# Clears and weight pieces moved within the second attention, and score products made twice in half of its maxima pass

## The reference, cut to what matters

```python
h = h + _L1_attn_ref(_layernorm(h), W_attn, b_attn, P_q, P_k, P_v, W_back, W_proj, b_proj)
h = h + _L1_ffn_ref(_layernorm(h), Wr, W1, b1, W2, b2, sW1, sb1, sW2, sb2)
# attention: 12 heads of 8, causal
qkv = x @ W_attn + b_attn; q, k, v = split(qkv); q = q @ P_q; k = k @ P_k; v = v @ P_v
w = softmax(mask(q @ k.T / sqrt(8))); out = (w @ v) @ W_back @ W_proj + b_proj
# experts: 8 experts (192 -> 768 -> 192), top 2 of them for each token, and a shared one
```

## Time and profile before

| | us |
|---|---|
| median of the runs (3) | 943.63 |
| lowest, highest | 940.45, 945.43 |
| the profiled execution, its own time | 941.8 |
| its span in the trace | 939.9 |
| TensorE busy | 687.7 (73%) |
| VectorE busy | 648.5 (69%) |
| ScalarE busy | 647.2 (69%) |
| GpSimd busy | 315.0 (34%) |

### The profile page before, as it was taken

One profiled execution on the slowest core, in us unless ns is written; L12 is line 12 of the kernel. 1 busy time (PEld: TensorE's weight loads), 2 busy tenths in 40 slices (PEclk: granted clock), 3 DMA queues, 4 the chain that ended last, 5 costly groups with the idle time before them and its releaser, 6 DMA issues. The chain is left out here.

```text
span 939.9 us, 19804 instructions
## 1 busy us (share of the span) xinstructions
PE 687.7 (73%) x7422; PEld 517.9 (55%) x7423; DVE 648.5 (69%) x1374; ACT 647.2 (69%) x1225; POOL 315.0 (34%) x252
## 2 busy tenths in 40 slices
PE   2586472344199555989999939745985898999995
PEld 2563240122177323479999924333554567999994
DVE  3478998999679888955454455467669885554542
ACT  1568955999799686876556437889774752977672
POOL 6730750000000000067887442510002102678854
PEclk9887555555599776999999969765997899999998
DMA  6444772000032224933443261830554942334432
GB/s 200 145 89 119 242 252 52 0 17 9 3 110 93 93 84 147 331 90 69 64 59 54 31 205 56 312 110 3 201 209 150 339 179 75 59 59 64 60 39 30
DMA packets 61367, 105.78 MB, mean 113 GB/s; under 512 B 9709, under 2 KB 43128, under 8 KB 61032
## 3 DMA queue, kind: packets, MB, share of 16 engines
q1 hardware_dynamic: 44904, 88.19, 28.2%
q0 software_dynamic: 16384, 16.53, 11.4%
HBM read 76.91 MB, written 27.77 MB: 111 GB/s over the span
## 5 line engine op out<-in xcount | busy, mean ns | idle before, releaser
L2414 DVE SCALAR_TENSOR_TENSOR m_hT<-m_pu,m_unit,m_hT 128x512 f16<-128x512 f32 (+1 forms) x138 | 86.3, 663 | 21.5 <-ACT m_hT L2370 21.5
L1140 ACT ACTIVATE a_ex<-m_pieces,a_nb 128x256 bf16<-128x256 f16 x192 | 94.3, 492 | 5.4 <-DVE a_nb L1166 5.4
L2377 ACT ACTIVATE m_pu<-m_pu,m_b,m_unit 128x256 f32<-128x256 f32 (+1 forms) x138 | 63.7, 507 | 45.0 <-PE m_pu L2284 43.1
L2406 DVE COPY m_xgT<-m_px 128x768 f16<-128x768 f16 (+1 forms) x46 | 22.9, 497 | 102.9 <-PE m_px L2252 100.2
L979 PE MATMUL a_pp<-a_room 16*128 16x256 bf16 x240 | 56.1, 412 | 39.4 <-DVE m_pieces L1154 31.9
L2370 ACT ACTIVATE m_hT<-m_pu,m_unit 128x512 f16<-128x512 f32 (+1 forms) x138 | 81.3, 634 | 0.0
L2213 POOL DMA_INDIRECT m_xg<-xn_d,m_token x70 | 68.9, 984 | 32.3 <-issue 19.4
L2381 ACT ACTIVATE m_pu<-m_pu,m_unit 128x512 f32<-128x512 f32 (+1 forms) x69 | 41.1, 596 | 52.0 <-PE m_pu L2284 51.9
L2225 POOL DMA_INDIRECT out_h<-m_yo,m_token x39 | 62.1, 1592 | 31.6 <-DVE m_yo L2424 12.0
L2225 POOL DMA_INDIRECT h_d<-m_yo,m_token x39 | 62.1, 1591 | 25.5 <-issue 9.7
L2284 PE MATMUL m_pu<-m_xgT,m_pieces 128*128 128x256 f16 (+1 forms) x690 | 69.3, 260 | 0.9 <-DVE m_xgT L2406 0.9
(11 more groups left out here) (492 smaller groups left out, 1691.1 us busy)
## 6 DMA issues: line engine op xcount, KB each, us to landing
m_pieces<-in_m_w SPq DMA_DIRECT2D x11, 768.0 KB, 5.0
a_early_w<-in_m_w SPq DMA_DIRECT2D x10, 768.0 KB, 5.5
hv_raw<-in_m_w SPq DMA_DIRECT2D x8, 768.0 KB, 8.1
w1h_d<-hv_parts SPq DMA_DIRECT2D x8, 768.0 KB, 5.0
m_w<-w1h_d SPq DMA_DIRECT2D x8, 768.0 KB, 9.4
m_pieces<-in_m_w SPq DMA_DIRECT2D x8, 576.0 KB, 5.9
a_room<-in_m_w SPq DMA_DIRECT2D x8, 576.0 KB
hv_raw<-in_m_w SPq DMA_DIRECT2D x8, 576.0 KB, 7.8
```

Source lines behind the costliest of these rows:

```text
L1140: last = act.activation(ex[:, n % 2, r], v16t[:, n, r, :], ACT.Exp, bias=nbt[:, n, r:r + 1], scale=scale, accum_out=sumst[:, n, r:r + 1])
L2377: act.activation(pu[:, u, n, q * w:(q + 1) * w], pu[:, u, n, q * w:(q + 1) * w], ACT.Relu, bias=b1[:, bass.ds(e * FC + 2 * n + q, 1)], sca ...
L2414: last = v.scalar_tensor_tensor(hT[:, u, 1, third], pu[:, u, n, 0:2 * w], unit[:, 1:2], hT[:, u, 0, third], ALU.mult, ALU.subtract)
```

## The change

1. The third clear of `vv` waits for `normed` at 8 and no longer at 12.
2. FRONT - 1 becomes FRONT in the projection block: store, fetch and GpSimd's `low` of piece 6 (and the fetch of piece 10) move there from the maxima block, `low` of piece 6 ahead of `weigher.reduce`.
3. In the maxima block, units 12 to 23 make the 8 score products twice; the second set starts over, so the result is the same.
4. In the context block VectorE splits pieces 7 and 8 ahead of its wait for the turned late rows, and SyncE stores them (and fetches 11 and 12) ahead of `put_rows` and `take_rows`. The splits of pieces 9 to 15 stand behind the division of images 0 to 6 and no longer between the copy and the division.

```diff
-    COUNT, FRONT, RAW, PARTS = 2 * E, 7, 4, 3
+    COUNT, FRONT, MIXED, RAW, PARTS = 2 * E, 7, 9, 4, 3
...
-                        for n in range(Halves.FRONT - 1):
+                        for n in range(Halves.FRONT):
                             halves.store(sp, n)
                             halves.fetch(sp, n + 4)
...
-                            pool.wait_ge(normed, 4 * k + 4)
+                            pool.wait_ge(normed, min(4 * k + 4, 8))
                             pool.memset(vv[:, t0:t1], 0.0).then_inc(cleared, 1)
...
-                        for n in range(Halves.FRONT - 1):
+                        for n in range(Halves.FRONT):
                             halves.low(pool, n)
                         weigher.reduce(pool)
...
-                            halves.store(sp, Halves.FRONT - 1)
-                            halves.fetch(sp, Halves.FRONT + 3)
                             sp.wait_ge(kept, 2)
...
-                        @block.gpsimd
-                        def _(pool):
-                            halves.low(pool, Halves.FRONT - 1)
...
-                                for qt in range(2):
-                                    for hh in range(4):
+                                for again in range(2 if n >= ALL // 2 else 1):
+                                    for qt in range(2):
+                                        for hh in range(4):
...
+                        for n in range(Halves.FRONT, Halves.MIXED):
+                            halves.store(sp, n)
+                            halves.fetch(sp, n + 4)
                         sp.wait_ge(kept, 3)
                         put_rows(sp, 1)
                         take_rows(sp, 1)
-                        for n in range(Halves.FRONT, Halves.COUNT):
+                        for n in range(Halves.MIXED, Halves.COUNT):
...
+                        for n in range(Halves.FRONT, Halves.MIXED):
+                            halves.split(dve, n)
                         dve.wait_ge(rest_turned, 1)
                         v.tensor_copy(top_rows(LATE, B), rest).then_inc(kept, 1)
-                        for n in range(Halves.FRONT, piece):
-                            halves.split(dve, n)
                         for img in range(B):
...
-                            if img < B - 1:
-                                halves.split(dve, piece + img)
                             dve.wait_ge(turned, img + 1)
...
+                            if Halves.MIXED + img < Halves.COUNT:
+                                halves.split(dve, Halves.MIXED + img)
```

More of the change, by code:

```diff
@@ L3187, in score @@
                                     pe.wait_ge(kept, TURNS[n - 2] // 2 + 1)
-                                for qt in range(2):
-                                    for hh in range(4):
[L3190 to L3194, removed]
+                                for again in range(2 if n >= ALL // 2 else 1):
+                                    for qt in range(2):
+                                        for hh in range(4):
+                                            r0, at0 = 32 * hh, img * S
+                                            nc.tensor.matmul(pa[:, j, hh, qt * P:(1 + 2 * qt) * P],
+                                                             qs[r0:r0 + KS, g, at0 + qt * P:at0 + (qt + 1) * P],
+                                                             ks[r0:r0 + KS, g, at0:at0 + P * (qt + 1)],
+                                                             start=(qt == 0), stop=(n >= ALL // 2 and again == 0 and qt == 1))
                                 for b in range(4):
@@ L3312, in _ @@
                         v = nc.vector
-                        piece = Halves.COUNT - B + 1
                         narrow(dve, LAST)
```

## The result

The kernel after runs in 945.22 us (median of 22 runs, 941.06 to 950.63), the kernel before beside it in 941.88 (22 runs, 940.01 to 946.59). The ratio is 1.0026, 95% interval 1.0014 to 1.0039: slower by 2.5 us (1.3 to 3.7) by the ratio; the two medians lie 3.3 apart. The forecast was 0.7 us less. The profiled execution of after has a span of 944.7 us against 939.9 before, 4.8 more, somewhat above the typical pair.

What follows compares the result with a forecast made beforehand. ScalarE was taken to bound the projection and maxima blocks, read block by block. Terms 0.0 - 1.1 + 0.2 - 0.1 + 0.3 gave -0.7 us on 943.63, so 942.9 us, range 937.5 to 946.5.

Steps and rivals of the forecast that it cites:

- The failed step: Projection block: two of four normalisations held behind piece 0's `low`, quarter 2.7 us late, ScalarE's end 6.3 us earlier.
- the bound of 4.0: Projection block: ScalarE's gain of 4.0 us if normalisations are held behind `low` of pieces 0 and 1 both.
- rival C: Projection block: GpSimd holds VectorE's normalisations longer, all-reduce 2.3 us later; total +2.8 us, 946.4; chance 0.18.
- The all-reduce behind its library: Projection block: with piece 6 ahead, the all-reduce waits the full 5.95 us for its library, starting at 614.8 as before.
- The term of 5.95: Projection block: library load ahead of the all-reduce, at most 5.95 us in the trace, charged in full.
- Rival A: Projection block: all-reduce library mostly hidden or short, or VectorE held less; total -5.2 us, 938.4; chance 0.22.
- "The block's end moves by 0.0": Projection block: ScalarE's 6.3 us gain all turns into a library wait before the all-reduce, so no net change.
- Maxima: Maxima block: -1.1 us as the 2.99 us fold and ScalarE's hole go, +0.2 us for doubled products.
- rival B: Maxima pass: doubled products raise TensorE's clock, which holds into the context block; -3.6 us more, 939.3; chance 0.08.
- Context: Context block: TensorE gaps at images 0 and 1 go, -2.3 us; piece 15 before the last copy, +2.2; sum -0.1.
- Experts: Experts' block: a library load of 7.0 to 10.1 us delays the router's split; +0.3 us (0 to 1.5).
- The range: Whole kernel: 937.5 to 946.5 us, lower end from the hidden-or-short-library and raised-clock cases, upper end from longer-held normalisations.

Runs made afterwards that it cites:

- e9_clearfree: Kernel before with the third clear early and `low` of pieces 0 and 1 waiting for 12 and 16 normalisations; ratio to before 0.9918.
- e10_gap: Kernel after with only `low` of piece 1 waiting until 16 normalisations are done; ratio to before 0.9998.
- e1: Kernel before with only the third clear of the second projection block moved earlier; ratio to before 0.9984.
- e6: Kernel after with `low` of piece 6 made by VectorE instead of GpSimd; ratio to before 0.9951.
- e7: Kernel after with the split of piece 15 back between the copy and the turned scores of image 6; ratio to before 0.9994.
- e8: Kernel after with one added GpSimd scaling of one column in the maxima block, to bring its arithmetic library back early; ratio to before 1.0020.
- e2: Kernel before with only store, fetch and `low` of piece 6 moved ahead of the all-reduce; ratio to before 1.0055.
- e3: Kernel before with only the score products of the maxima pass's second half made twice; ratio to before 0.9997.
- e4: Kernel before with only the context block's new order: pieces 7 and 8 ahead of the row wait, piece 15 behind the turned scores; ratio to before 0.9989.
- e5: Kernel after with `low` of pieces 0 and 1 waiting for 12 and 16 normalisations; ratio to before 0.9946.
- best2: Kernel before with early third clear, both `low` waits and the new context order, piece 15 ahead of the turned scores; 931.72 us, ratio 0.9893.
- best: Kernel after without doubling, with both `low` waits, piece 6's `low` on VectorE, piece 15 ahead of turned scores, one-column GpSimd scaling; 931.11 us, ratio 0.9884.

## Why the prediction was wrong, point by point

- **The failed step** is "I let two of the four fall behind the 3.1 us of `low`: the quarter is normalised at about 577.5, 2.7 late", and with it "TensorE turns it 2.7 late, ScalarE has used up its 1.6 and 1.0 more. So ScalarE's end moves by 7.3 - 1.0 = 6.3 us". ScalarE won 2.3 us, below even the bound of 4.0 that I gave for both pieces. Two things in this step were wrong.
- **Its first error, the hold**: both `low` held a normalisation, and the quarter ended 4.0 us late against the block's start. The mechanism was in the text as rival C; I had put two instructions behind the first `low` and none behind the second.
- **Its second error, the clock**: I had charged TensorE nothing but the delay. Its granted clock fell to 0.50 behind the hold, and the 36 products took 2.6 us longer (10.53 - 7.96); the hole of 1.97 us is part of that. The 4.0 and the 2.6 are 6.6 of the 6.9 us that lie between the free gain (9.2, e9_clearfree) and the 2.3. e10_gap shows the second error apart: its quarter is 2.7 late, as forecast, its products take 1.2 longer, and ScalarE wins 4.9 and not 6.3; the block ends 1.4 later, and the total is unchanged. The clock fell at these products in all six profiles with a held quarter (for 10.2 us in after, 6.8 in e1, e6, e7 and e8, 3.4 in e10) and in none of the eight without. That the standstill lowers it is my reading of this coincidence; no run has the one without the other. The four of these that keep the hole of 7.29 us (before, e2, e3, e4) have such a fall later, behind that hole (10.2 us from about 590 in before), and there ScalarE shows no gap.
- **The all-reduce behind its library**: right, and the sign of the whole hangs on it. The term of 5.95 (its own numbers give 5.97) was near: counted from MODIFY_POOL_CONFIG as there, it is 5.8 to 6.0 us in e2, e5, e7, e8 and e10, and 6.0 to 6.3 from the end of the last `low`. So in before it was hidden with nothing to spare: the all-reduce started 6.2 us after the `low` of piece 5. In the profile of after it was 7.4 by that count; the other kernels lack these extra 1.3 us, no second profile of after tells whether they are usual, and their cause was not found. Rival A (library hidden or short) is refuted by e2_piece6.
- **"The block's end moves by 0.0"** failed through the first step alone: 68.6 in e7 and e8 is 4.0 later than before, which is the 6.3 that piece 6 costs (e2) less the 2.3 that ScalarE won. The library's extra 1.3 makes it 5.3 in the profile of after.
- **Maxima**: forecast -1.1 and +0.2, measured -1.0 (e2) and +0.4. Right.
- **Clock by doubling** (rival B): refuted, granted 0.50 to the end of the pass and beyond.
- **Context**: the two gaps went and 2.60 us at the last turn came, as forecast; the sum looks 1 us too high (VectorE ends 1.1 earlier in after and 1.4 in e4, not 0.1). Most of that is a third gap in the profile of before, 0.83 us at 684.87, which no releaser explains and which is 0.3 in e1 and e2 and absent in e3 and e9 with the same order. What I missed is the clock: with the order of before it fell to 0.50 once more at the second of the two gaps, for 3.4 us in e1 and e2 and 6.8 in e9, though not in before and e3; with the new order, in none of nine profiles. So the new order may be worth more than the profile of before shows.
- **Not foreseen**: the output block's clock. From VectorE's end in the context block to the router's first product it is 26.5 us in before, e3 and e9, with transposes of 1.92. It is 27.56 in e1, e4 and e8, which have the library in place as well but slow transposes: 1.1 us. In best2 it is 28.4, with the clock at 0.50 for 6.8 us instead of 3.4. Whether the change causes it stays open. With the context order of before it fell in e1 and e2 (3.0 and 3.1 us of transposes) and not in before, e3 and e9; with the new order it fell in all nine profiles (3.2 to 3.6), those of e7 and the candidates too.
- **Experts**: forecast +0.3 (0 to 1.5). From the last transposes (L1831) to the router's first product it is 0.59 to 0.60 us wherever the library is in place, and with a load 0.96 in e6, 1.3 in e5, e7 and e10, 1.67 in after and 1.70 in e2: 0.4 to 1.1. The price lies in the range given; in the profile of after it was 1.07, and there the five small instructions behind the load took 3.7 us (729.98 to 733.66).
- **The range**: its lower end of 937.5 does not follow from its own numbers, for A with B beside it would be 938.4 - 3.6 = 934.8. Nothing hangs on that: 945.2 lies within it. It is the direction that was wrong.

The Trainium skill, "Advanced Engine Details and Errata", VectorE Performance Modes, says that GpSimd and VectorE's two-port modes block each other. By that rule the normalisations are held, and the trace agrees: 3.25 us for a normalisation of 0.38. Its table gives TENSOR_TENSOR no two-port mode, so the fold of L3131, which the prediction counted as agreeing, was held (2.99 us) outside of that rule.

## What to carry to other kernels

When an instruction of GpSimd is moved earlier, look at which VectorE instruction stands at its new time, and charge one hold for each GpSimd instruction in a row, not one for the group; then look at what the held one feeds, and count every hop behind it, with TensorE's clock: here a wait of 4.85 us was followed by products at 0.50. A library change that is hidden behind a wait for data is free only while the last instruction of the old library is off that wait's path: moving one `low` of 3.1 us there moved the block's end by 6.3 us. Where a part gains by itself and another loses, run them apart: here the gain of 8 us in the early clear was hidden by two losses that two waits and one piece left in its place undo.

## What the runs showed of the hardware that I had not expected

- Of two subtractions of GpSimd in a row each held one normalisation of VectorE to its end (3.25 us for the first held one in after); where only one was in the way, one normalisation took 2.58 and three took 0.37.
- Behind such a hold TensorE's granted clock was at 0.50 for 3.4 to 10.2 us (six profiles), and the same 36 products took 9.1 to 10.5 us instead of 7.96.
- The all-reduce took 1.76 us instead of 0.37 when VectorE made a subtraction from SBUF beside it (e6_veclow; 1.66 in `best`).
- The change back to the arithmetic library took 6.8 to 7.2 us in the projection block and 9.2 to 10.1 beside the experts' transfers (721.99 - 712.8 in e6_veclow, 732.87 - 722.8 in e2_piece6). The DMA share was 0.00 and 0.19 in the first case (e2, after) and 0.78 to 0.79 in the second. The change to the all-reduce's library took 5.8 us at a share of 0.77 (e7_tail), so not every load is longer beside transfers.
